# Narrow attention: dividing the outputs on VectorE through 32x32 block transposes, without the trip of the sums through DRAM

## The reference

```python
scores = einsum("bqhd,bkhd->bhqk", q, k) * scale      # 1024 x 1024, scale = 16 ** -0.5
probs = softmax(scores, axis=-1)                      # causal in the first of the two
out = einsum("bhqk,bkhd->bqhd", probs, v)
```

## Time and profile before

| what | value |
|---|---|
| median of 3 runs | 3053.86 us (3051.91 to 3058.37) |
| the profiled execution's own time | 3051.21 us |
| its span, first to last instruction | 3049.6 us |
| mean granted TensorE clock | 0.877 |
| TensorE, VectorE, ScalarE, GpSimd busy | 80%, 53%, 36%, 32% |
| a0: first maximum, last copy of psO, last store issued | 175.96, 460.03, 476.4 us |
| a5: the same | 2263.03, 2650.65, 2667.1 us |

### The profile page before, as it was taken

The page is one execution under the profiler, slowest core; times in us unless marked ns, Lnnn a source line. Parts: engine busy times, 40 slices in busy tenths (PEclk is TensorE's granted clock), DMA queues, the critical chain, the costliest instruction groups (busy, mean ns, idle before and its releaser), DMA issues. The chain is left out here.

```text
span 3049.6 us, 46851 instructions
## 1 busy us (share of the span) xinstructions
PE 2429.3 (80%) x15980; PEld 1328.7 (44%) x15980; DVE 1606.1 (53%) x2586; ACT 1105.7 (36%) x1987; POOL 990.8 (32%) x914
## 2 busy tenths in 40 slices
PE   3759994575799698799999997856739999747996
PEld 3614433234688566233333332733512222146885
DVE  3867743536333332566666663443768989353223
ACT  1326671241000233244444444124206888611221
POOL 0532232200222111477777775110360122203331
PEclk7969997666799899799999999967868999967998
DMA  3442312431565466222222221553351121014555
GB/s 108 98 84 65 82 34 61 86 64 60 161 213 189 159 187 180 67 82 85 84 77 81 83 82 43 146 85 83 81 101 51 46 60 41 17 62 144 196 195 181
DMA packets 255409, 305.22 MB, mean 100 GB/s; under 512 B 66222, under 2 KB 200532, under 8 KB 254740
## 3 DMA queue, kind: packets, MB, share of 16 engines
q1 hardware_dynamic: 222836, 228.64, 26.1%
q0 software_dynamic: 30496, 72.95, 9.2%
q10 hardware_dynamic: 1920, 1.57, 0.3%
HBM read 210.47 MB, written 91.78 MB: 99 GB/s over the span
## 5 line engine op out<-in xcount | busy, mean ns | idle before, releaser
L1718 DVE TENSOR_REDUCE a_mxw<-a_rows 128x2 f32<-128x1024 f32 (+1 forms) x448 | 480.5, 1106 | 110.3 <-PE a_rows L1574 63.0
L1693 ACT ACTIVATE a_probs<-a_cols 128x512 f32<-128x512 f32 (+3 forms) x896 | 445.8, 550 | 214.7 <-PE a_cols L1616 138.4
L2120 DVE TENSOR_REDUCE a_mxw<-a_rows 128x2 f32<-128x1024 f32 x256 | 313.3, 1224 | 210.5 <-PE a_rows L1958 208.8
L2098 ACT ACTIVATE a_probs<-a_cols 128x1024 f32<-128x1024 f32 x256 | 261.9, 1025 | 268.8 <-PE a_cols L1987 251.0
L1939 POOL TENSOR_TENSOR a_sums<-a_sums,a_probs 128x1024 f32<-128x1024 f32 x128 | 309.7, 2419 | 97.4 <-ACT a_probs L2098 84.7
L1616 PE MATMUL a_cols<-a_qs,a_ks 50*128 50x512 bf16 (+7 forms) x1792 | 279.2, 365 | 23.9 <-DMA a_qs<-a_nparts 12.2
L2374 PE MATMUL e_psU<-e_xT,e_w 128*128 128x256 f32 x1216 | 273.9, 384 | 1.9 <-ACT e_xT L2421 1.2
L500 PE MATMUL t_psP<-t_xT,t_wf 128*128 128x256 f32 x1024 | 240.2, 392 | 36.2 <-ACT t_xT L568 13.0
L1983 PE MATMUL a_cols<-a_qf,a_kf 64*128 64x512 f32 x1024 | 267.5, 600 | 0.0
L1644 PE MATMUL a_out<-a_probs,a_vs 128*17 128x256 f32 (+4 forms) x3328 | 257.4, 383 | 0.2 <-ACT a_probs L1693 0.2
L2374 PEld LDWEIGHTS e_psU<-e_xT,e_w 128*128 128x128 f32 x1216 | 234.4, 193 | 35.6 <-ACT e_xT L2421 1.6
(11 more groups left out here) (249 smaller groups left out, 2956.6 us busy)
## 6 DMA issues: line engine op xcount, KB each, us to landing
e_w<-in_w SPq DMA_DIRECT2D x69, 512.0 KB
e_w<-in_w SPq DMA_DIRECT2D x30, 1024.0 KB
qk_wide_scratch<-t_f SPq DMA_DIRECT2D x32, 512.0 KB, 2.9
q_scratch<-t_parts POOLq DMA_DIRECT2D x128, 96.0 KB, 2.4
a_qs<-q_scratch SPq DMA_DIRECT2D x96, 128.0 KB
a_qs<-q_scratch SPq DMA_DIRECT2D x168, 64.0 KB, 2.4
a_ks<-k_scratch SPq DMA_DIRECT2D x144, 64.0 KB, 2.6
vw_scratch<-t_v SPq DMA_DIRECT2D x16, 520.0 KB, 5.9
```

The lines of the kernel that those rows point to most:

```text
L1693: act.activation(pr[ug % RING][:, 2 * hp + e, c0:512], psC[(2 * at + e) % 3][:, 0:512 - c0], ACT.Exp, scale=scale).then_inc(ex_done, 1)
L1718: dve.tensor_reduce(mxw[w][:, a, :, hp, t % 4:t % 4 + 1], src[:, :, 0:n], AX.X, ALU.max).then_inc(s_free, 1)
L2098: act.activation(pr[i][:], psC[i % 2][:], ACT.Exp, scale=scale).then_inc(ex_done, 1)
L2120: dve.tensor_reduce(mxw[:, j % 2, :, j // 2:j // 2 + 1], psR[:], AX.X, ALU.max).then_inc(s_free, 1)
```

## The change

The sums no longer leave the core. When a unit's values are in psO, VectorE transposes it by 32x32 blocks from PSUM into `turned` (128 partitions by 16 blocks by 32): query rows now lie on partitions, a head's 16 features and its sum in the columns of a block. It inverts the 16 sums of each partition (128 x 16), multiplies the 16 x 16 features by them into `divided`, and transposes `divided` back by blocks into `on`. GpSimd only issues the stores, once both units are there. The new `turn_out` (transpose, reciprocal) stands in VectorE's order at the slots `due[LAG - 1]` and `due[UNIT0 + LAG - 1]`, that is ahead of the slot that TensorE issues right behind the unit's last values; `divide` (multiply, transpose back) follows after one slot of the maxima. psO is free for the next unit's values after the first transpose (o_turned). ScalarE's copies, GpSimd's `exchange` and multiply, the buffers osb, rec, sums and inverses and the DRAM scratch go away. `divided` is zeroed once by VectorE at the start of the stage, and GpSimd's memset of rec goes.

```diff
-def narrow_attention_stage(nc, G, tag, *, q, k, v, o, sums, causal=False):
+def narrow_attention_stage(nc, G, tag, *, q, k, v, o, causal=False):
...
         pr = [st.sb(f"probs{r}", [P, H, 512]) for r in range(RING)]
-        osb = [st.sb(f"osb{p}", [P, S]) for p in range(3)]
-        rec = st.sb("rec", [P, S])
+        turned, divided = st.sb("turned", [P, 16, 32]), st.sb("divided", [P, 16, 32])
+        inverse = st.sb("inverse", [P, 16, 1])
         on = [st.sb(f"on{p}", [P, S]) for p in range(3)]
-        sm, inv = st.sb("sums", [P, H * S // P]), st.sb("inverses", [P, H * S // P])
         mxw = [st.sb(f"mxw{w}", [P, 2, 2, H // 2, QT // 2]) for w in range(2)]
...
         st_ready, ex_done, pv_done = st.sem("cols_ready"), st.sem("exp_done"), st.sem("pv_done")
-        o_copied, rec_done, o_done = st.sem("out_copied"), st.sem("sums_inverted"), st.sem("out_done")
-        sums_out, sums_in = st.sem("sums_out"), st.sem("sums_in")
-        inv_out, inv_in = st.sem("inverses_out"), st.sem("inverses_in")
+        o_turned, o_done = st.sem("out_turned"), st.sem("out_done")
         stored = [st.sem(f"stored{p}") for p in range(3)]
...
                     load_rest(pool, 1, which)
-                pool.memset(rec[:], 0.0)
-                pool.drain()
-
-                def exchange(g):
-
-                    p = g % 3
-                    pool.wait_ge(o_copied, 2 * (g + 1))
-                    pool.dma_start(sums[0, p % 2].rearrange("(h t) -> h t", h=H), osb[p][hd:P:32, :]).then_inc(sums_out, 16)
-                    pool.wait_ge(sums_out, 16 * (g + 1))
-                    pool.dma_start(sm[:], sums[0, p % 2].rearrange("(p x) -> p x", p=P)).then_inc(sums_in, 16)
-                    pool.wait_ge(rec_done, g + 1)
-                    pool.dma_start(sums[1, p % 2].rearrange("(p x) -> p x", p=P), inv[:]).then_inc(inv_out, 16)
-                    pool.wait_ge(inv_out, 16 * (g + 1))
-
-                    wait(pool, o_done, g)
-                    for h in range(H):
-                        pool.dma_start(rec[32 * h:32 * h + hd, :],
-                                     sums[1, p % 2, h * S:(h + 1) * S].partition_broadcast(hd)).then_inc(inv_in, 16)
                 for g in range(NG):
                     p = g % 3
-                    exchange(g)
-
-                    pool.wait_ge(inv_in, 16 * H * (g + 1))
-
-                    wait(pool, stored[p], g // 3 * H * 16)
-                    pool.tensor_tensor(on[p][:], osb[p][:], rec[:], ALU.mult).then_inc(o_done, 1)
-                    pool.wait_ge(o_done, g + 1)
+                    pool.wait_ge(o_done, 2 * (g + 1))
                     for h in range(H):
...
-                        wait(pe, o_copied, 2 * g + w)
+                        wait(pe, o_turned, 2 * g + w)
                     mid = (c0 + 512) // 2
...
             def _(act):
-                def copy_out(g, w):
-
-                    act.wait_ge(pv_done, g * NUG + unit_end[w])
-                    if w == 0:
-
-                        wait(act, o_done, g - 2)
-                    act.activation(osb[g % 3][:, 512 * w:512 * (w + 1)], psO[:], ACT.Copy).then_inc(o_copied, 1)
-
                 act.wait_ge(ones_set[0], 1)
...
                                            scale=scale).then_inc(ex_done, 1)
-                        if n == LAG - 1 and g:
-                            copy_out(g - 1, 1)
-                        if n == UNIT0 + LAG - 1:
-                            copy_out(g, 0)
-                copy_out(NG - 1, 1)
...
                 dve.memset(psO[:], 0.0).then_inc(out_zeroed, 1)
+                dve.memset(divided[:], 0.0)
                 if causal:
...
-                def invert_sums(g):
-                    dve.wait_ge(sums_in, 16 * (g + 1))
-
-                    wait(dve, inv_out, 16 * g)
-                    dve.reciprocal(inv[:], sm[:]).then_inc(rec_done, 1)
+                def turn_out(g, w):
+
+                    dve.wait_ge(pv_done, g * NUG + unit_end[w])
+                    dve.transpose(turned[:].rearrange("p b f -> p (b f)"), psO[:]).then_inc(o_turned, 1)
+                    dve.drain()
+                    dve.reciprocal(inverse[:], turned[:, :, hd:hd + 1])
+
+                def divide(g, w):
+
+                    dve.drain()
+                    dve.tensor_tensor(divided[:, :, 0:hd], turned[:, :, 0:hd], inverse[:].broadcast_to([P, 16, hd]), ALU.mult)
+                    dve.drain()
+                    wait(dve, stored[g % 3], g // 3 * H * 16)
+                    dve.transpose(on[g % 3][:, 512 * w:512 * (w + 1)], divided[:].rearrange("p b f -> p (b f)")
+                                  ).then_inc(o_done, 1)
...
                     slots, due = body(g), plan(g)
-                    at = due[(UNIT0 + LAG + 4) if causal else (UNIT0 // 2 + 2)]
-                    for s, slot in enumerate(slots):
-                        if g and s == at:
-                            invert_sums(g - 1)
-                        run(slot)
-                    if g and at >= len(slots):
-                        invert_sums(g - 1)
-                invert_sums(NG - 1)
+                    todo = ([(due[LAG - 1], g - 1, 1)] if g else []) + [(due[UNIT0 + LAG - 1], g, 0)]
+                    turned_unit = None
+                    for s in range(len(slots) + 1):
+                        while todo and todo[0][0] == s:
+                            if turned_unit:
+                                divide(*turned_unit)
+                            turned_unit = todo.pop(0)[1:]
+                            turn_out(*turned_unit)
+                        if s < len(slots):
+                            run(slots[s])
+                            if turned_unit:
+                                divide(*turned_unit)
+                                turned_unit = None
+                    if turned_unit:
+                        divide(*turned_unit)
+                turn_out(NG - 1, 1)
+                divide(NG - 1, 1)
...
-    a16 = dict(q=Q16, k=K16, v=V16, o=OA, sums=SU)
+    a16 = dict(q=Q16, k=K16, v=V16, o=OA)
```

More of the change, by code:

```diff
@@ L2569, in decoder @@
     OA = nc.dram_tensor("attn_scratch", (HEADS // 4, 2 * B, 64, 512), F32, kind="Internal").ap()
-    SU = nc.dram_tensor("sums_scratch", (2, 3, 4 * S), F32, kind="Internal").ap()
     SW = nc.dram_tensor("sums_wide_scratch", (2, 2, 4, 512), F32, kind="Internal").ap()
```

## The result

The changed kernel took 3043.04 us (median of 7 runs, 3034.61 to 3048.34), the kernel before 3056.8 (7 runs, 3051.35 to 3059.68): ratio 0.9955, 95% interval 0.9941 to 0.9968, that is 13.8 us faster (9.8 to 18.0). The forecast was 3044 and -9.5 us. The profiled execution has span 3043.5.

A forecast was written before the change was run, and what follows sets the result against it. TensorE was taken as the bound inside a0 and a5, with the GpSimd and DRAM chain on the path at their ends. Terms -23.6 + 8.3 + 5.5 + 0.3 = -9.5 us gave 3044 us, range 3036 to 3061.

The forecast's parts named there:

- ends, to the issue of the stores: Ends of a0 and a5: the chain to the store issue falls from 14.29 and 14.40 us to 2.56, saving 23.6.
- a5: hand-overs: Between units in a5: VectorE's added work holds TensorE 0.53 at thirteen regular hand-overs, 1.5 at the first; +8.3 us.
- a0: hand-overs: In a0: 0.9 late per regular group, 2.0 in the first, small gains between groups and in the last; +5.5 us.
- memset of divided: Start of a0 and a5: zeroing `divided` ahead of VectorE's first maxima, taken as +0.3 us in all.
- the stepping through of one unit: One a5 hand-over stepped forward: 2.19 us of VectorE work holds TensorE's next rows but one by 0.53 us.
- The first hand-over: First hand-over in the packed stretch: VectorE idles only 0.7, so 1.5 us lost in a5; a0's first group 2.0.
- the rival of the falling clock: TensorE's clock falls at the holds, seven a0 hand-overs at 2.3 us each, +16, total +6.6: 3060 us; chance 0.14.
- The copy: ScalarE's 0.60 us output copy at each hand-over: removing it gains 0.14 us per unit, not 0.41 or 0.60.
- The same four store DMAs follow in both kernels: Stage ends, behind the store issue: the prediction's statement that the same four stores follow; no gain counted there.
- Transposes at double price: Both VectorE transposes of each unit: four-byte blocks at half rate, 1.22 us each, sum +14.6: 3068 us; chance 0.11.
- Larger holds: Hand-overs: VectorE's reserve smaller than its idle suggests, 0.35 more at each of 21, +7: 3051 us; chance 0.17.
- All hidden: Hand-overs: buffers let VectorE catch up without a hold, only ends and 0.14 to 0.2 a unit count: 3027; chance 0.06.

The follow-up runs named there:

- e2_last_only: The kernel before, with only the last group's two units of each stage turned and divided by VectorE: 3028.0 us, ratio 0.9896.
- e3_divide_late: The changed kernel with multiply and second transpose later among the maxima (7 slots in a5, 2 in a0, instead of 1): 3026.56 us, ratio 0.9897.
- e1_drain: The changed kernel with one more GpSimd drain, ahead of its wait for the last group's outputs: 3029.82 us, ratio 0.9915.
- e5_copies: The kernel with the late divide, plus a ScalarE copy of a constant 128x512 block at each hand-over: 3030.79 us, ratio 0.9914.
- e6_before_drain: The kernel before with one more GpSimd drain, ahead of the last group's exchange, nothing of the change: 3041.79 us, ratio 0.9951.
- e4_turn_twice: The changed kernel with the first transpose done twice, 0.78 us more on VectorE per unit: 3065.83 us, ratio 1.0031.

## Why the prediction was right

Each term, as forecast and as the profile after has it:

```
                                   forecast   measured
ends, to the issue of the stores    -23.6      -23.4   (2.63 each)
a5: up to the first hand-over         --        -2.6   (not in the prediction)
a5: hand-overs                       +8.3       +9.6   (regular 0.53 | 0.54; first 1.5 | 2.6)
a0: hand-overs                       +5.5       +6.6   (group +0.7 | +0.83, one +1.18; first 2.0 | 2.7; last -0.7 | -1.4)
memset of divided                    +0.3       not on the path, 0.48
GpSimd's drains at the ends           --        -5.1   (not in the prediction)
sum                                  -9.5      -14.9
a0 and a5 by the records                       -15.1   (322.7 to 315.1, 426.9 to 419.4)
medians                                        -13.8   (-9.8 to -18.0)
```

- **The ends** were sized by the nearest rows and are right to 0.1 us each. That the gain of the shorter chain lies there, e2_last_only shows by making only that part of the change.
- **The regular hand-over in a5** is right in size and in place; the stepping through of one unit gave the held rows within 0.02 us. That the order, and not the amount of work, makes the hold is shown by e3_divide_late. The prediction did not ask this question, and it was worth about as much as the change itself (14.7 us by the records, against 15.1).
- **The first hand-over** of a5 was forecast at 1.5. The same loop gave 1.1 in e1_drain, and 2.6 in the profile after, where the clock fell behind it; that profile had its first hand-over 2.6 us earlier, so that the second one stands 98.3 us behind the start of a5 in both kernels. The forecast was near what the change costs there, and the 1.5 on top is the rival of the falling clock, at one hand-over and in one of two profiles. In a0 the first was too cheap, 2.0 for 2.7: TensorE waits 1.7 us longer there (2.62 for 0.95), and the clock comes back to 1.00 later, behind this hand-over in both profiles of the loop. e3_divide_late, with the clock back 7.3 us behind it, has 26.8 for 29.15, against 26.5 before. What of the 2.7 is the clock's was not separated.
- **In a0** the net of a regular group was forecast at 0.9 - 0.2 = 0.7 and came to 0.83, but it is made up otherwise: behind the hand-over inside the group 0.68 is lost (343.38 - 321.17 = 22.21, against 21.53 between the copies of before) and behind the one between groups 0.16 (10.61, against 10.45), where a gain of 0.2 was forecast. That the two errors cancel is luck. Most of the last group's gain is no gain of the change that the runs show: its last interval went from 16.70 to 15.43 us, and in the profile before the clock was 0.50 there (446 to 448 us), in the one after 1.00. Of kernels that keep the copies, e2_last_only has 15.43 too, with the clock at 1.00.
- **The copy** at 0.14 a unit is shown by e5_copies (0.17).
- **The missed term** is GpSimd's drain. "The same four store DMAs follow in both kernels" was true and was taken to mean that nothing behind them changes. e1_drain and e6_before_drain show that it does: what stands behind them depends on how many DMAs GpSimd has issued before. The hand-overs' total was right, +13.8 forecast and +13.6 measured with the start of a5 (-2.6 + 9.6 + 6.6), so the missed 5.1 are nearly all of the distance between -9.5 and -14.9. (The 0.26 us of the prediction for the old reciprocal is 0.34 in the trace; it is in no term.)
- **The time** of 3044 us came closer to 3043.04 than the gain of 9.5 to 13.8, by luck: the forecast started from the 3053.86 of three runs, and the kernel before that the result stands against has 3056.8.
- **The rivals.** Transposes at double price: out (0.70 and 0.71). The falling clock: once, behind the first hand-over of a5, for 1.5 us where the rival took 2.3 for each fall, and not at the hand-overs inside the groups of a0, where the rival had put it (at a0's first one it only comes back later); a0 gets it at 0.8 us more a unit (e4_turn_twice). Larger holds: in a regular group of a0 by 0.1, in a regular unit of a5 not. All hidden: not as written, but reached by e3_divide_late, whose a5 units are 0.15 shorter than before.

In the profiled executions only 6.1 us lie between the spans (3049.6 and 3043.5). Stages without an edit hide the rest: a1 and a4 were 4.2 and 8.2 us longer in the one after, a5 and a0 7.5 and 7.7 shorter (from the records of the trace). One execution each is not enough for this kernel's total; the stage is what to read.

## What to carry to other kernels

Work added to an engine that two others pace themselves by can cost by where it stands in its order more than by how long it takes (2.2 us cost 0.54 at one place, and nothing at another; 0.78 more at the bad place cost 0.8): step one hand-over forward, find the instruction that is held, and ask how many slots later the work could stand before you give up the change. Where a stage ends in a barrier, look past the last store to the first instruction of the next stage in both kernels: what a queue has issued in the whole stage may be paid for there. Where one interval of a profile stands out, read the granted clock in it, and the same interval in another execution of the same loop, before you book it to the change. And undo the change everywhere except where its gain is (here the last group); what is left of the difference is its cost.

## What the runs showed of the hardware

- GpSimd's drain at the end of a0 and a5 lies on the path and took about 0.08 us for each DMA that GpSimd had issued since its last drain: 7.25 us for 91, 4.72 for 57, 0.95 for 12. At other stages' ends 80 DMAs went with 3.17 us, and 32 with 2.67 or with 0.22, so the number alone does not set it. Taken while GpSimd is idle anyway the drain costs nothing that shows: -14.3 us for one added line (e6_before_drain).
- VectorE's transpose of 32x32 blocks of four-byte data, 128x512: 0.70 us from PSUM and 0.71 from SBUF, the price of a copy from PSUM (0.69) and not that from SBUF (0.43).
- TensorE's granted clock fell to 0.50 in mid-stage at waits of 1.5 us at a hand-over, in most groups of e4_turn_twice (a group's 452 matmuls 2.7 us longer, 32.61 for 29.88) and once in the profile after. Waits of the same length passed without it in another group of e4_turn_twice (1.51) and in e1_drain (1.46). In the groups of a0 in the changed kernel, with waits of 0.63 to 0.98, it stayed at 1.00.
